# Two edits in a gated attention and expert kernel: where the ternary steps of the last four tiles stand in the order, and who splits the first shared weights between the routing stage's transposes

## The reference

```
x = x + tanh(g_xattn[0]) * L0_xattn(layernorm(x), ctx, mask)   # 16 heads of 32, sigmoid gate, masked softmax
x = x + tanh(g_ffn[0])   * L0_ffn(layernorm(x))                # ternary weights, rows quantised to 127 steps
x = x + tanh(g_xattn[1]) * L1_xattn(layernorm(x), ctx, ctx)    # sigmoid(Q^T K / sqrt(128)), one head
x = x + tanh(g_ffn[1])   * L1_ffn(layernorm(x))                # 16 experts, 4 of them per token, and two shared ones
```

## Time and profile before

| | |
|---|---|
| runs shown | 1298.67 us median of 3 (1297.68 to 1304.92) |
| profiled execution | 1298.22 us, its span 1296.5 us |
| PE busy | 1215.9 us, 94% |
| DVE, ACT, POOL busy | 668.9, 575.7, 430.9 us |
| 0 to 422 us | first attention's heads, with the ternary step of the first tiles |
| 422 to 549 us | end of the heads, second attention, ternary step of the last tiles |
| 549 to 602 us | routing stage, up to the last group's hidden rows |
| 602 to 1296 us | shared expert and routing, then the expert tiles |

### The profile page before, as it was taken

How to read it: one execution, slowest core, us unless ns; L and a number is a source line. 1 busy time by engine, 2 the same in 40 slices (tenths; PEclk the granted TensorE clock), 3 DMA queues, 4 the chain that set the end, 5 groups by cost and what they waited for, 6 DMA issues and landing times. The chain is left out here.

```text
span 1296.5 us, 25673 instructions
## 1 busy us (share of the span) xinstructions
PE 1215.9 (94%) x7824; PEld 1026.1 (79%) x7836; DVE 668.9 (52%) x1410; ACT 575.7 (44%) x1384; POOL 430.9 (33%) x518
## 2 busy tenths in 40 slices
PE   6998999999999789988999998999999999999995
PEld 6877778788787567666777786889998989999995
DVE  6556545555545799843666644542233553424241
ACT  4555456356356668763121111543334553434342
POOL 1102211210213466340004761244434444343433
PEclk9999999999999889979999999999999999999998
DMA  9100000000000003022000221765446666645554
GB/s 334 36 17 20 18 1 20 18 1 18 17 18 1 26 26 108 8 107 100 1 1 1 91 108 59 249 165 90 76 76 148 176 150 153 146 81 135 86 140 73
DMA packets 54335, 100.36 MB, mean 77 GB/s; under 512 B 5094, under 2 KB 21990, under 8 KB 54262
## 3 DMA queue, kind: packets, MB, share of 16 engines
q0 software_dynamic: 15824, 37.76, 15.5%
q1 hardware_dynamic: 38438, 61.65, 14.7%
HBM read 72.91 MB, written 26.48 MB: 77 GB/s over the span
## 5 line engine op out<-in xcount | busy, mean ns | idle before, releaser
L1876 PE MATMUL t_H<-m_W,t_xT 128*128 128x352 f32 x1632 | 280.2, 327 | 6.4 <-DVE m_W L1954 4.9
L1876 PEld LDWEIGHTS t_H<-m_W,t_xT 128*128 128x128 f32 x1632 | 261.6, 188 | 9.6 <-DVE m_W L1954 7.5
L1844 POOL DMA_INDIRECT out_dram<-t_ys,t_sid x68 | 109.6, 1612 | 220.4 <-ACT t_ys L1905 107.3
L1921 ACT ACTIVATE t_sl<-t_H 128x352 f32<-128x352 f32 x68 | 31.6, 464 | 174.0 <-PE t_H L1876 174.0
L722 ACT ACTIVATE pr<-SC,neg 128x128 f32<-128x128 f32 x256 | 89.9, 377 | 38.2 <-DVE neg L927 38.2
L46 PE MATMUL t_Y<-m_W,t_hT 128*128 128x512 f32 (+1 forms) x207 | 87.4, 422 | 5.2 <-issue 3.1
L1999 DVE TENSOR_TENSOR t_hT<-t_TH,t_hT 128x384 fp32r<-128x384 f32 x68 | 37.8, 556 | 101.9 <-ACT t_hT L1942 100.8
L1905 ACT ACTIVATE t_ys<-t_Y,t_wcol 128x512 f32<-128x512 f32 x69 | 47.4, 687 | 93.7 <-PE t_Y L48 93.7
L1975 DVE TENSOR_TENSOR t_h<-t_H,t_sl 128x352 f32<-128x352 f32 x68 | 35.5, 523 | 102.5 <-ACT t_sl L1921 102.2
L48 PE MATMUL t_Y<-m_W,t_hT 128*128 128x512 f32 (+1 forms) x207 | 81.8, 395 | 0.0
L47 PE MATMUL t_Y<-m_W,t_hT 128*128 128x512 f32 (+1 forms) x207 | 81.5, 393 | 0.0
(11 more groups left out here) (474 smaller groups left out, 3225.6 us busy)
## 6 DMA issues: line engine op xcount, KB each, us to landing
m_raw<-in_L_ffn_w_dram SPq DMA_DIRECT2D x28, 704.0 KB, 5.2
m_raw<-in_L_ffn_w_dram SPq DMA_DIRECT2D x14, 512.0 KB, 6.5
rows_d<-before_w SPq DMA_DIRECT2D x17, 256.0 KB, 2.0
CT<-in_ctx_dram SPq DMA_DIRECT2D x8, 512.0 KB, 3.7
X<-in_x_dram SPq DMA_DIRECT2D x4, 1024.0 KB, 13.9
out_dram<-X SPq DMA_DIRECT2D x3, 1024.0 KB, 4.3
m_raw<-in_L_ffn_w_dram SPq DMA_DIRECT2D x14, 192.0 KB, 6.4
CT<-in_ctx_dram SPq DMA_DIRECT2D x8, 256.0 KB, 2.7
```

What stands on the lines that cost most here:

```text
L1844: pool.indirect_dma_start(out=m["out_rows"][:, :], out_offset=bass.IndirectOffsetOnAxis(ap=sid[:, b:b + 1], axis=0), in_=ys[:, b, :], in_o ...
L1876: x_ = pe.matmul(bk[b % 2][:, 0:I], xT[:, b % 2, jx, k, :], W13[:, jw, k, j, :], start=k == 0 and jx == jw, stop=k == KC - 1 and jx == 1)
```

## The change

In the plan, the words of the last group's tail are ordered anew: `aT.0` stands ahead of `rd.0` and `bc.3`, `aS.0.2` ahead of `oP.3`, and `uT.1 fm.1` (tile 13) leave the heads. The table `between` puts tile 13's `uT` at slot 2 and its `fm` at slot 4, and the steps of tiles 12 to 15 that stood in slots 0 to 20 into slots 3 to 30; `ta` to `tc` move too. In the routing stage DVE takes over the four low parts of the first shared weights behind its low parts of tiles 0, 1, 5 and 6; `hidden` can do one half alone, and the halves stand behind the transposes of the third and fourth tile of each group, `logit_rows` behind the second half.

```
-            "oP.2 rb.0 pv.6 pT.14 rc.3 aS.0.0 pT.15 rd.0 bc.3 aT.0 pv.7 on.3 oT.3 u.0 aS.0.1 ag.0.0 aT.1 ag.0.1 "
-            "oP.3 uT.0 u.1 aS.0.2 fm.0 uT.1 fm.1 ", NG - 1)
-        between = {0: "sf.-4", 1: "st.-2", 2: "sf.-3", 3: "st.-1", 5: "ra.-1", 6: "rb.-1", 7: "rd.-1 u.-2", 9: "uT.-2", 10: "u.-1",
-                   12: "fm.-2", 13: "uT.-1", 16: "fm.-1", 18: "sf.-2", 20: "sf.-1", 22: "ta.1", 24: "tb.1", 26: "tc.1", 28: "sw", 36: "ta.2", 40: "tb.2",
-                   42: "tc.2", 52: "ta.3", 56: "tb.3", 58: "tc.3"}
+            "oP.2 rb.0 pv.6 pT.14 rc.3 aS.0.0 pT.15 aT.0 rd.0 bc.3 pv.7 on.3 oT.3 u.0 aS.0.1 ag.0.0 aT.1 aS.0.2 ag.0.1 "
+            "oP.3 uT.0 u.1 fm.0 ", NG - 1)
+        between = {2: "uT.-3", 3: "sf.-4", 4: "fm.-3 st.-2", 6: "st.-1", 8: "ra.-1 sf.-3", 10: "rb.-1", 12: "rd.-1 u.-2", 17: "uT.-2",
+                   18: "u.-1", 20: "fm.-2", 23: "uT.-1", 25: "sf.-2", 26: "fm.-1", 28: "sw", 30: "sf.-1", 32: "ta.1", 34: "tb.1", 36: "tc.1",
+                   44: "ta.2", 48: "tb.2", 50: "tc.2", 52: "ta.3", 56: "tb.3", 58: "tc.3"}
...
-        FIRST_SPLIT_AT = (1, 4, 5)
+        FIRST_SPLIT_AT, FIRST_LOW_AT = (1, 4, 5), (0, 1, 5, 6)
...
             def _(pool):
-                for n in range(PARTS):
-                    if n == 2:
-                        row_power(pool, c, scales, slice(3 * GB, NB), powered)
-                    raw, hi, lo = part(0, n)
-                    pool.wait_ge(w_hi, n + 1)
-                    pool.tensor_tensor(lo, raw, hi.bitcast(F32), ALU.subtract).then_inc(w_lo, 1)
+                row_power(pool, c, scales, slice(3 * GB, NB), powered)
...
-                def hidden(q):
+                def hidden(q, halves=(0, 1)):
...
-                    for W_, bk in ((W1[b], A[q % 2]), (W3[b], B[q % 2])):
+                    for W_, bk in [((W1[b], A[q % 2]), (W3[b], B[q % 2]))[n] for n in halves]:
...
-                    x_.then_inc(ab_fill, 1)
+                    if 1 in halves:
+                        x_.then_inc(ab_fill, 1)
...
-                        hidden(t // GB - 1)
+                    if t % GB == 2 and t > GB:
+                        hidden(t // GB - 1, (0,))
+                    if t % GB == 3 and t > GB:
+                        hidden(t // GB - 1, (1,))
                         logit_rows(t // GB - 1)
...
-                def split_lo(n):
-                    raw, hi, lo = part(1, n)
-                    dve.wait_ge(w_hi, PARTS + n + 1)
+                def split_lo(n, b=1):
+                    raw, hi, lo = part(b, n)
+                    dve.wait_ge(w_hi, PARTS * b + n + 1)
...
+                    if t in FIRST_LOW_AT:
+                        split_lo(FIRST_LOW_AT.index(t), 0)
```

## The result

The changed kernel takes 1291.3 us (median of 7, 1290.9 to 1292.6), the kernel before beside it 1304.7 us (median of 7, 1297.7 to 1306.3); the ratio is 0.9913, 95% interval [0.9894, 0.9933]. The forecast was 1282.0 us with a range of 1276 to 1291: the sign is right, the size is not. Profile against profile the time fell from 1298.22 to 1291.16 us, the span by 7.0 us.

The account below looks back on a forecast made before the run. The prediction took TensorE (PE), busy for 94% of the span, as the bound, with gains only where it waits or its clock drops. 8.6 us in A plus 7.8 in B made 16.4, from 1298.22 to 1282 us, range 1276 to 1291.

Parts of the forecast that it names:

- Place A: End of the heads and first slots of the second attention: 13.75 us lost, 5.1 of new waits, gain 8.6 us.
- The pace of DVE and POOL in slots 2 to 8: Second attention's loop: the step on which the forecast said most depends; no size of its own.
- The end of the heads: Before tile 15's output projection: of PE's 1.65 us wait for the low part of oT, 0.4 us stays.
- Slot 4.: Second attention: ap.1.0 waits until DVE has emptied aO.0's bank; 1.5 us, bounds 0 and 2.
- Slot 5.: Second attention: aS.2.0 waits for tile 2's low part, behind two adds on POOL; 1.3 us, bounds 0 and 2.
- Tiles 14 and 15.: Second attention: the 3.75 us wait for quantised tile 14 goes; late low parts cost 1.2 us, bounds 0 and 2.5.
- waits in A only move: Rival: DVE's and POOL's queues set the pace of slots 2 to 20, A gives nothing; 1290.4 us, chance 0.16.
- The clock in A: Heads' end and second attention's start: 5.2 us of slow clock behind two waits, to go away with them.
- clock stays low in A: Rival: new waits hold the clock at its lower level from slot 2 to 20; 1304 us, chance 0.04.
- Place B: Routing stage: covered waits between transposes and DVE making the low parts gain 7.8 us (5.5 to 8.4).
- Products between transposes: Routing: halves of hidden cover PE's waits around transposes; 4.3 + 3.2 us gained, 0.5 lost to switches.
- Low parts by DVE: Start of routing: DVE takes POOL's four subtracts, its 3.16 us stand goes, first gate earlier; 0.8 us (0.2 to 1.2).

Follow-up runs that it names:

- the late quantise: Changed kernel with tile 15's quantise behind tile 14's ternary product (slot 20, not 18), tile 15's ternary product at slot 28, not 26: 1288.3 us.
- the low parts by POOL: Changed kernel with routing's four subtracts and the power back on POOL in the order of before, products between transposes kept: 1295.1 us.
- the tail alone: Kernel before with only the new order of the heads' tail, routing as before: 1301.5 us, ratio interval [0.9964, 1.0004].

## Why the forecast was wrong

**Place A, the new waits: 5.1 us forecast, 11.8 found (the kernel before had 2.3 of the same kinds), and the clock on top.** The pace of DVE and POOL in slots 2 to 8, on which the prediction said that most depends, held: aO.2 is 9.6 us earlier. The waits that the change was to remove did go. The end of the heads came as forecast (0.51 us for 0.4), but for 1.20 us at the ternary product of tile 12, which the sum left out. Then:

- *Slot 4.* "I bound it by 0 and 2, and take 1.5." The mechanism (a lone `fm` between two emptyings makes the next tile's product use the bank that DVE is still to empty) was right and the wait is 1.08 us. It was priced once; the plan puts a lone `fm` in two more such places, slots 20 and 26, and there it cost 2.67 and 1.01 us. At the first, DVE's quantise of tile 15 stood ahead of the emptying; the edit that moves it behind, and the product at slot 26 to 28, brought 3.0 us back.
- *Slot 5.* "Bounds 0 and 2, I take 1.3": 0.72 for ks.2, 0.5 for ks.3.
- *Tiles 14 and 15.* "The adds of tiles 14 and 15 move in POOL's queue past two and three further tiles' ks; waits of under a microsecond for these are there already, and I leave them." This is the step that failed: it puts these places in POOL's queue at nothing, and the two powers, which the new order has behind ks.3, it does not price at all. What stands ahead of ks.4 on POOL is the second power of the scales, which waits 1.69 us for DVE; POOL's rows of the changed kernel:

```profile
453.92 1.21 POOL L421 TENSOR_TENSOR tmp<-tmp,nhalf 128x2 f32<-128x2 f32 x1 [1.69 <-DVE tmp L762]
455.09 1.15 POOL L440 CAST Wk<-CT 128x512 fp32r<-128x512 f32 x1
```

So ks.4 is late, and PE waits 2.26 us for it. One of the adds that were left at nothing, that of tile 15, waits 3.68 us for DVE ahead of ks.8 (it starts at 489.23), and PE waits 1.50 us. Without the power in the way, though, the end stayed where it was (1287.7 us for 1288.3). The reading below these terms was wrong too: each wait was priced by itself, as if DVE and POOL had time to spare behind it. DVE is busy for 93% of 442 to 482 us, and two of its four groups shown above stretch beside POOL; four edits, each of which took something out of the way, only exchanged one wait for another. It is the first rival, "waits in A only move", 1290.4 us with a chance of 0.16. What spoke for it, the quantise stretched to 4.22 us, weighed more than the 7 us of undisturbed PE time held against it: there (442 to 452 us of the kernel before) DVE was busy for 84% and POOL for 53%, in the next 10 us for 97% and 71%. That DVE and POOL have no time to spare is shown by these exchanges and by the run with the subtracts cut; what part of it is work and what part the stretching beside each other is not.

**The clock in A.** Forecast as going away with its two waits. It did, and came back behind the two new ones: 5.2 us before, 3.3 after. The rival "clock stays low in A" did not happen; it fell for nine products at a time.

**Place B** was right in mechanism and near in size: 8.8 us for 7.8. Products between transposes: 6.1 to 6.5 us for a forecast of 4.3 + 3.2 - 0.5 = 7.0. Low parts by DVE: 2.2 us for 0.8 (0.2 to 1.2), the term that was mis-sized. Its mechanism, an earlier gate of the first group, gave 1.3 us where it had 1.2 at most; the rest is mainly the clock, which it did not count and which came back up four products earlier (0.7 us). The 0.45 us set against it, for a power and a subtract that go one after the other, is in no run: beside the power at 552.64 the subtract of 1408 columns takes 1.62 us, as in the earlier trace rows. DVE did not become the bound. "So the gain is carried to the end" failed by 2.5 us, 1.56 of them clock at the first expert products.

The range has a slip: by the bounds given for slots 4, 5 and 14 the new waits can be 2.5 us more, not 4.0.

So 16.4 us forecast became 0.7 + 8.8 - 2.5 = 7.0.

## What to carry to other kernels

Where two engines that slow each other are both near full under a third engine's products, the price of moving a step is not the wait it removes: add up both engines' work in the new order, with the stretched durations, and see whether it fits. Of the edits here that went on from the late quantise, the only one whose executions all lie below its took work off them (a cast given to ScalarE), and even that gave nothing in another order. When a mechanism has been found at one place of a plan, look for every other place where the new order makes it. And price a wait of PE together with the products behind it, since one of 2 us may cost 1.7 us more.

## What the runs showed of the hardware

- The same wait of PE can be followed by either clock. 2.28 and 2.66 us in A were followed by products 0.23 us apart in one kernel, 2.26 and 2.67 us by nine products 0.43 us apart in another; at the first expert products a wait of 1.5 us was followed by 4.10 us in the kernel before, 4.11 in the one with the low parts by POOL, and 5.66 us in the changed kernel. No run here tells what decides. At the expert products it goes with the routing: of ten profiles with the whole routing edit eight have 5.66 us or 5.67, and none of the four without DVE's low parts (the kernel before twice, the tail alone, the low parts by POOL) has. Why is not shown, as the wait of 1.5 us ahead of them is the same in all fourteen. The Trainium skill, TensorE: Matmul & The Clock Gate, Part 1, calls the warm-up variable from run to run; these rows show the like in the middle of a kernel.
- With GpSimd's subtracts over 512 columns, 1.3 to 1.8 us each, cut to 8 columns the second attention ends 12.1 us earlier, although PE's waits for them sum to only 5.3 us. Beside them DVE's instructions that read two SBUF tiles last longer (0.68 to 1.78 us, on 128x2 elements 0.15 to 1.25 us); the two groups that read PSUM keep 744 and 688 ns.
- With these subtracts cut, a tile of the second attention takes PE 5.93 us (490.92 to 532.45 us for seven), against 6.44 us (499.46 to 544.51) in the changed kernel: 3.5 us over these seven tiles, in a stretch where PE's listed waits sum to 0.8 us. The other 8.5 us of the 12.1 lie ahead of it.
